# Second sweep of a two-layer graph network: one edge scalar moves from a one-hot matrix to the turned edge features

## The reference, cut to what matters

```python
w = ssp(edge_attr @ W_f1) @ W_f2 * (ssp(s0 @ W_s1) @ W_s2)
w1, w2, w3, w4 = jnp.split(w, 4, axis=-1)          # 128 columns each
x0e, x1e = split_irreps(x[edge_src])               # 128, and 3 x 128
sh0, sh1 = (edge_sh[:, 0], edge_sh[:, 1:4])        # 1 and 3 scalars of the edge
out0 = w1 * x0e * sh0[:, None] + w4 * (jnp.einsum('eum,em->eu', x1e, sh1) / jnp.sqrt(3.0))
out1 = w2[:, :, None] * x0e[:, :, None] * sh1[:, None, :] + w3[:, :, None] * x1e * sh0[:, None, None]
out = jax.ops.segment_sum(merge_irreps(out0, out1), edge_dst, num_segments=N)
```

## Time and profile before

| | |
|---|---|
| time, median of 3 runs | 1228.67 us (1228.24 to 1230.1) |
| profiled execution: its own time, its span | 1229.83 us, 1228.1 us |
| busy share of the span: PE, PEld, DVE, ACT, POOL | 81%, 52%, 70%, 43%, 64% |
| second sweep alone, 700 to 1100 us: PE, DVE, ACT, POOL busy | 396.21, 350.98, 241.75, 278.65 us of 400 |
| granted PE clock there | 1.00 |

### The profile page before, as it was taken

The page is one execution under the profiler, slowest core; times in us unless marked ns, Lnnn a source line. Parts: engine busy times, 40 slices in busy tenths (PEclk is TensorE's granted clock), DMA queues, the critical chain, the costliest instruction groups (busy, mean ns, idle before and its releaser), DMA issues. The chain is left out here.

```text
span 1228.1 us, 23671 instructions
## 1 busy us (share of the span) xinstructions
PE 995.1 (81%) x5530; PEld 642.5 (52%) x5531; DVE 854.4 (70%) x2190; ACT 533.3 (43%) x1559; POOL 780.0 (64%) x809
## 2 busy tenths in 40 slices
PE   2316556199999996756999999999999999999974
PEld 1213232055555554643666666666666666666653
DVE  7351101177778775744888888888888888888857
ACT  2203121023222333543665666656566555666631
POOL 3777777577777760116676776767667676676721
PEclk9757668699999997886999999999999999999987
DMA  9201011277877780125545545455454555545302
GB/s 346 76 15 33 25 32 50 75 238 238 242 240 241 240 218 17 60 94 180 171 156 165 163 153 171 150 167 161 157 170 148 170 159 159 166 150 167 127 1 86
DMA packets 109167, 177.46 MB, mean 145 GB/s; under 512 B 40191, under 2 KB 79343, under 8 KB 109009
## 3 DMA queue, kind: packets, MB, share of 16 engines
q0 software_dynamic: 33184, 130.15, 33.5%
q1 hardware_dynamic: 72752, 45.60, 12.4%
q10 hardware_dynamic: 3200, 1.38, 0.5%
HBM read 157.31 MB, written 19.74 MB: 144 GB/s over the span
## 5 line engine op out<-in xcount | busy, mean ns | idle before, releaser
L1038 POOL TENSOR_TENSOR dot<-ring,ed 128x768 f32<-128x768 f32 x88 | 129.6, 1473 | 134.1 <-issue 109.8
L698 PE MATMUL ps<-ring,aw 128*128 128x512 f32 x352 | 195.6, 643 | 17.7 <-DVE aw L649 16.3
L1028 POOL DMA_INDIRECT ring<-tab_d,ed x176 | 170.4, 968 | 62.2 <-issue 30.5
L618 POOL DMA_INDIRECT ring<-xt_d,ed x176 | 167.5, 952 | 61.4 <-issue 42.0
L375 POOL DMA_INDIRECT slots_d<-stage,stage_pos x157 | 153.5, 978 | 66.3 <-issue 48.7
L1067 PE MATMUL ps<-mm_sb,ohs 128*128 128x512 f32 x352 | 189.1, 619 | 1.4 <-DVE acc L1197 1.4
L1069 PEld LDWEIGHTS ps<-mm_sb,ohs 128*128 128x128 f32 x1056 | 145.6, 191 | 84.2 <-issue 84.2
L1122 ACT ACTIVATE ohs<-oh,ed 128x128 f32<-128x128 f32 x528 | 172.6, 394 | 0.0
L1152 ACT ACTIVATE S_sb<-ps 128x512 f32<-128x512 f32 x176 | 95.5, 595 | 134.6 <-PE ps L1109 134.6
L1069 PE MATMUL ps<-mm_sb,ohs 128*128 128x128 f32 x1056 | 146.2, 275 | 0.0
L1175 DVE TENSOR_TENSOR ps<-S_sb,ps 128x1024 f32<-128x1024 f32 x88 | 108.2, 1229 | 28.0 <-ACT S_sb L1152 26.8
(11 more groups left out here) (194 smaller groups left out, 1859.0 us busy)
## 6 DMA issues: line engine op xcount, KB each, us to landing
ilb<-f_d SPq DMA_DIRECT2D x88, 128.0 KB, 3.8
ed<-slots_d SPq DMA_DIRECT2D x176, 38.0 KB, 3.8
tab_d<-tabrow SPq DMA_DIRECT2D x5, 896.0 KB, 3.7
slots_d<-fill SPq DMA_DIRECT2D x8, 418.0 KB, 4.3
f_d<-ft SPq DMA_DIRECT2D x88, 38.0 KB
ring<-xt_d,ed POOLq DMA_INDIRECT x176, 4.0
hcat<-f_d SPq DMA_DIRECT2D x176, 16.0 KB, 3.8
ring<-tab_d,ed POOLq DMA_INDIRECT x176, 4.4
```

The costliest lines, as they stand in the source:

```text
L618: gp.indirect_dma_start(xg[:, c, k, :], None, xt_d[:, :], bass.IndirectOffsetOnAxis(ap=ed[:, c, k, JD:JD + 1].bitcast(I32), axis=0))\
L698: pe.matmul(ps[:, 2 * u, :], aw[:, r, k, :], xg[:, c, k, 0:D], start=(k == 0), stop=(k == 1))
L1028: gp.indirect_dma_start(xj[:, r, k, :], None, tab_d[:, :], bass.IndirectOffsetOnAxis(ap=ed[:, c, k, JD:JD + 1].bitcast(I32), axis=0))\
L1038: gp.tensor_tensor(dot[:, u, :, :, :], xj[:, r, :, P:D].rearrange("p k (m n) -> p k m n", m=3), ed[:, c, :, IL + 2:IL + 5].unsqueeze(3).to ...
```

## The change

- The scalar `sh0` leaves the one-hot. SP now also loads `s0b`, the turned scalar of each edge spread over 32 rows, and loads `hcat` in one transfer instead of two. A new DVE stage `scaled_features` (lag 2, first in the list) multiplies the turned features by it into `hs0`.
- The columns of `w2` are put in the order w1, w3, w2, w4, in 16 small loads instead of 4 (`NLOADS` 20 to 32). `factors` makes the first 256 columns of F from `hs0` and the last 256 from `hcat`: two matmuls of 512 columns and four of 256.
- `messages` has four steps: the w1 and w2 parts as before, then the inner term (in place in `psF`), then the w3 part, then an addition of the inner term to the first 128 columns.
- `sums` uses the plain one-hot for the 512 columns and drops the separate matmul of 128 columns for the inner term. DVE no longer builds `ohs[..., 0, :]`.

```diff
-        ohs = sb("ohs", [P, 2, 2, SH, P], scope=sweep2)
+        s0b = sb("s0b", [P, U, P], scope=sweep2)
+        hs0 = sb("hs0", [P, 2, P], scope=sweep2)
+        ohs = sb("ohs", [P, 2, 2, SH - 1, P], scope=sweep2)
...
-                        load(w2[HID * q:HID * q + HID, :], W_s2 if q < 2 else W_f2)
+                        w_ = W_s2 if q < 2 else W_f2
+                        for to, fro in ((0, 0), (1, 2), (2, 1), (3, 3)):
+                            load(w2[HID * q:HID * q + HID, P * to:P * to + P], w_[:, P * fro:P * fro + P])
...
-                    for k in range(2):
-                        sp.dma_start(hcat[HID * (k + 2):HID * (k + 3), c, :], turned[k, 0:EA, :]).then_inc(ed2[c], 16)
+                    sp.dma_start(hcat[2 * HID:P, c, :], turned[:, 0:EA, :]).then_inc(ed2[c], 16)
+                    sp.dma_start(s0b[2 * HID:P, c, :], turned[:, IL + 1, :].unsqueeze(1).to_broadcast([2, EA, P])).then_inc(ed2[c], 16)
...
-                        pe.matmul(psA, ohs[:, u, k, 0, :], mm_sb[:, u, k, 0:D], start=(k == 0), stop=False)
+                        pe.matmul(psA, oh[:, u, k, :], mm_sb[:, u, k, 0:D], start=(k == 0), stop=False)
                         for m in range(3):
-                            pe.matmul(psA[:, P * (m + 1):P * (m + 2)], ohs[:, u, k, m + 1, :], mm_sb[:, u, k, D:D + P],
-                                      start=False, stop=False)
-                        mm = pe.matmul(psA[:, 0:P], oh[:, u, k, :], mm_sb[:, u, k, D + P:D + 2 * P], start=False, stop=(k == 1))
+                            mm = pe.matmul(psA[:, P * (m + 1):P * (m + 2)], ohs[:, u, k, m, :], mm_sb[:, u, k, D:D + P],
+                                           start=False, stop=(k == 1 and m == 2))
...
+                    pe.wait_ge(hs_ready, g + 1)
...
-                        mm = pe.matmul((psS if q < 2 else psF)[:, q % 2, :], hcat[rows, c, :], w2[rows, :], start=True, stop=True)
+                        if q < 2:
+                            pe.matmul(psS[:, q, :], hcat[rows, c, :], w2[rows, :], start=True, stop=True)
+                        else:
+                            pe.matmul(psF[:, q - 2, 0:2 * P], hs0[rows, u, :], w2[rows, 0:2 * P], start=True, stop=True)
+                    for q in range(2, 4):
+                        rows = slice(HID * q, HID * q + HID)
+                        mm = pe.matmul(psF[:, q - 2, 2 * P:D], hcat[rows, c, :], w2[rows, 2 * P:D], start=True, stop=True)
...
-                    v.tensor_tensor(mm_sb[:, u, :, 0:D + P].rearrange("p k (s n) -> p k s n", n=P)[:, :, 0:5:4, :],
-                                    psF[:, :, 0:2 * P].rearrange("p k (s n) -> p k s n", n=P),
+                    v.tensor_tensor(mm_sb[:, u, :, :].rearrange("p k (s n) -> p k s n", n=P)[:, :, 0:5:4, :],
+                                    psF.rearrange("p k (s n) -> p k s n", n=P)[:, :, 0:3:2, :],
                                     xj[:, r, :, 0:P].unsqueeze(2).to_broadcast([P, 2, 2, P]), ALU.mult)
+
+                    v.wait_ge(dot_ready, g + 1)
+                    v.tensor_tensor(psF[:, :, 3 * P:D], psF[:, :, 3 * P:D], dot[:, u, :, 0, :], ALU.mult).then_inc(t_done, 1)
                     v.tensor_tensor(mm_sb[:, u, :, P:D].rearrange("p k (m n) -> p k m n", m=3),
-                                    psF[:, :, 2 * P:3 * P].unsqueeze(2).to_broadcast([P, 2, 3, P]),
+                                    psF[:, :, P:2 * P].unsqueeze(2).to_broadcast([P, 2, 3, P]),
                                     xj[:, r, :, P:D].rearrange("p k (m n) -> p k m n", m=3), ALU.mult)
-                    v.wait_ge(dot_ready, g + 1)
-                    v.tensor_tensor(mm_sb[:, u, :, D + P:D + 2 * P], psF[:, :, 3 * P:D], dot[:, u, :, 0, :], ALU.mult).then_inc(msg_ready, 1)
+                    v.wait_ge(t_done, g + 1)
+                    v.tensor_tensor(mm_sb[:, u, :, 0:P], psF[:, :, 3 * P:D], mm_sb[:, u, :, 0:P], ALU.add).then_inc(msg_ready, 1)
...
-                        v.tensor_scalar(oh[:, u, k, :], iota[:, :], ed[:, c, k, IL:IL + 1], None, ALU.is_equal)
-                        ins = v.tensor_scalar(ohs[:, u, k, 0, :], iota[:, :], ed[:, c, k, IL:IL + 1], ed[:, c, k, IL + 1:IL + 2],
-                                              ALU.is_equal, ALU.mult)
+                        ins = v.tensor_scalar(oh[:, u, k, :], iota[:, :], ed[:, c, k, IL:IL + 1], None, ALU.is_equal)
...
+                def scaled_features(g, c, n):
+                    u = c % 2
+                    v.wait_ge(ed2[c], n * 64)
+                    after(v, f_ready, g - 1)
+                    v.tensor_tensor(hs0[2 * HID:P, u, :], hcat[2 * HID:P, c, :], s0b[2 * HID:P, c, :], ALU.mult).then_inc(hs_ready, 1)
...
-                pipelined(v, (3, one_hot), (3, weights), (3, messages), (2, softplus), (0, turned_one_hot), (4, accumulate),
+                pipelined(v, (2, scaled_features), (3, one_hot), (3, weights), (3, messages), (2, softplus), (0, turned_one_hot), (4, accumulate),
```

More of the change, by code:

```diff
@@ L230, in batches @@
                 embed(q)
-        NLOADS = 20
+        NLOADS = 32
         loads = [0]
@@ L968, in build @@
         dot = sb("dot", [P, 2, 2, 3, P], scope=sweep2)
-        mm_sb = sb("mm_sb", [P, 2, 2, D + 2 * P], scope=sweep2)
+        mm_sb = sb("mm_sb", [P, 2, 2, D + P], scope=sweep2)
         ed2 = [sem(f"ed2_{c}") for c in range(U)]
@@ L991, in build @@
         w_done = sem("w_done")
+        hs_ready = sem("hs_ready")
+        t_done = sem("t_done")
         dot_ready = sem("dot_ready")
@@ L1121, in step @@
                         for k, m in which:
-                            ins = act.activation(ohs[:, u, k, m, :], oh[:, u, k, :], ACT.Copy, scale=ed[:, c, k, IL + 1 + m:IL + 2 + m])
+                            ins = act.activation(ohs[:, u, k, m - 1, :], oh[:, u, k, :], ACT.Copy, scale=ed[:, c, k, IL + 1 + m:IL + 2 + m])
                         if which[-1] == (1, 3):
```

## The result

The changed kernel takes 1213.61 us (median of 4 runs, 1212.89 to 1215.25) against 1228.7 us before (4 runs): 0.9877 of the time, interval 0.9862 to 0.9893, or 15.1 us less. The forecast was 1203.5 us, with a range of 1192 to 1218: the direction and the range held, the gain is 0.6 of the one predicted. The profiled execution took 1213.61 us, with a span of 1211.9 us (1228.1 before).

A forecast was written before the change was run, and what follows sets the result against it. Tied paths through PE's sums were taken to set 6.92 us an iteration; then a two-iteration path over DVE, 6.62: 0.30 x 87 = 26 us less, 1202.6, put at 1203.5 for mutual delays; range 1192 to 1218.

The forecast's parts named there:

- path A: One-iteration path inner, sums, accumulate, products, next inner: 6.93 us, called the pace before; 6.49 after the change.
- Path C: Two-iteration path: factors, ACT's copy of S, DVE's list, PE to the next-but-one factors: 13.24 us before, 13.23 after.
- Path E: Not predicted, drawn up later: inner, half 0 of sums, ACT's log steps, register read, accumulate, products: 6.92 before, 6.70 after.
- rival 2: The six matmuls of factors hand over badly, some 0.3 to 0.44 us: about 1213 to 1224 us; chance 0.12.
- rival 3: The row strips in factors no longer run side by side, adding 0.88 us: 1268 us; chance 0.06.
- D: Path of DVE's list of steps alone, one iteration: 5.91 us before, 5.92 after, no bound.
- rival 4: DVE and POOL block each other at scaled_features: 6.95 us an iteration, about 1231 us, no gain; chance 0.05.
- Rival 1: Only PE counts; the pace falls with sums alone by 0.44 to 0.55 us: 1181 to 1191 us; chance 0.07.

The follow-up runs named there:

- e5: The kernel before with the register read for accumulate moved ahead of weights: 1226.32 us, 0.9963 of the kernel before.
- e1: The changed kernel with the register read for accumulate moved ahead of weights: 1204.77 us, 0.979 of the kernel before.
- e3: The changed kernel with the register read moved ahead of weights and turned_one_hot moved behind products: 1193.49 us, 0.970 of the kernel before.
- e6: The kernel before with the 16 small loads of w2 in the old column order: 1230.51 us, 0.9998 of the kernel before.
- e8: The changed kernel with one more matmul of 128 columns in half 1 of sums: 1217.14 us, 0.9902 of the kernel before.
- e11: The kernel before with ACT's first log step (Abs) done twice: 1243.67 us, 1.0101 of the kernel before.
- e12: The changed kernel with early register read, turned_one_hot behind products and an own semaphore for the edge rows: 1191.09 us, 0.9674 of the kernel before.
- e9: The changed kernel with ACT's first log step (Abs) done twice: 1226.87 us, 0.9976 of the kernel before.
- e2: The changed kernel with turned_one_hot moved from ahead of accumulate to behind products: 1206.42 us, 0.9804 of the kernel before.
- e4: The changed kernel without the DVE addition of the inner term: 1211.7 us, 0.9846 of the kernel before.
- e7: The changed kernel with one more matmul of 128 columns in half 0 of sums: 1232.48 us, 1.0017 of the kernel before.
- e10: The changed kernel with the register read ahead of weights and ACT's first log step (Abs) done twice: 1200.29 us, 0.9754 of the kernel before.

## Why the prediction was right in sign and range, and wrong in size

*The step that failed* is the list of paths. "This path is the pace", said of path A, and "C takes over", said of the changed kernel, held only among the four paths listed, and none of them goes through ACT's log steps and the register read: what the read costs ahead of `accumulate` stood at nothing. The choice of A rested on the releaser printed beside `accumulate`, [0.46 <-PE ps L1071] in the earlier trace rows. That row names the wait of the instruction that came last by its semaphore, and the register read ahead of it, in the sequencer's rows, wasn't looked at. In the kernel before the two ended close together: the last L1071 ends by the model at 902.62, 0.17 before `accumulate`; the read's last row (SEQ_ASSERT) starts at 902.5, and one more register operation follows, as after the change. e5 says how close: without the read the pace falls by 0.05 us. After the change, counted from the end of the log, half 1 of `sums` ends 0.23 earlier (903.08 - 902.45 = 0.63 for 902.62 - 901.76 = 0.86), and `accumulate` still starts at 1.04 for 1.03, since the read takes as long as before. Path E, 6.70, stays above C, and the 0.22 of half 1 becomes idle time. 0.22 x 87 = 19 us is the gain inside the sweep (19.3 measured), where 0.30 x 87 = 26 stood in the sum. The start of the sweep, below, takes back another 4.2.

*That the range held is luck.* The forecast's own stretch was 1194 to 1211, and 1213.61 lies above it. The range reached up to 1218 only to take in a part of rival 2, and the bad hand-over of that rival did not happen.

*Path C* held as a sum. From the rows of the changed kernel it is 2.36 from `factors` (903.71) to `weights` (906.07), 4.13 to `accumulate` (910.20), 0.60, 1.01 and 5.31 (905.10 to 910.41): together 13.41, but for rounding the 13.40 of two iterations, with a gap of 0.21 ahead of `accumulate` in it (0.52 against 0.31 in e1). Without the gap, 13.19 / 2 = 6.60; e1 measured 6.594 and 1204.77 us, what had been forecast (6.62 and 1203.5) for the change itself. e3, which takes 0.31 more off C, gains 0.115 of the 0.155 that C gives. That C sets the pace in e1 rests on these two sums; no run adds a step to it there. Of the signs forecast for C, e1 shows that DVE no longer waits there and that PE waits for `products`. That `weights` waits longer than 0.32 for ACT's copy did not come: 0.19 on average in the changed kernel, 0.29 in e1.

*The terms.* Two matmuls, 0.22 each: right for half 0 (1.84 to 1.62), and for PE's stretch from `inner` to the next `factors` (5.77 to 5.31). `factors` with six matmuls: taken as 0.1, it measured 0.04 (1.21 to 1.25), so rivals 2 and 3 fell. PE's rows show why: L1122 starts at 904.26, 0.53 after L1119, as before the second four followed the first at 0.51. The Trainium skill, "TensorE: Matmul & The Clock Gate", Part 3 ("What overlaps and what doesn't"), says that a weight load overlaps a running matmul only on another row strip; by the prediction's estimate that would have made it 0.3 to 0.4. The trace does not agree, with 0.04. The addition and the inner term in place: 0.33 each, right. `scaled_features` takes 0.29 us (median of 88 is 290 ns) and 0.32 from its start to the next step's, for 0.20 in the sum of D, which set nothing. In the timeline POOL is at rest beside it, so rival 4 fell; the first of the 88, at 565.5 beside a POOL step of 1.47, took 0.69. The loads: 0, right (e6).

*Rival 1*, only PE counts, fell to e8: there PE does one matmul more in each iteration for 0.02 us.

*What the sum did not have* is the start of the sweep. The first `accumulate` comes 4.2 us later. SP's first load of the sweep and the first gather on POOL, after, then before:

```profile
550.66 0.37 SPq L1016 DMA_DIRECT2D ed<-slots_d  x1
556.54 0.98 POOL L1034 DMA_INDIRECT ring<-tab_d,ed  x1 [21.49 <-DMA s0b<-f_d]
```

```profile
550.51 0.37 SPq L1010 DMA_DIRECT2D ed<-slots_d  x1
555.21 0.98 POOL L1028 DMA_INDIRECT ring<-tab_d,ed  x1 [20.32 <-DMA hcat<-f_d]
```

The load is issued 0.15 later, and from it to the gather are 5.88 us for 4.70, 1.2 more: the first gathers wait for `s0b`, which shares a semaphore with `ed`. In the four kernels with the edge loads of before (before, e5, e6, e11) these are 4.6 to 4.7 us, in the nine with the shared wait 5.7 to 5.9, and in e12, where the gathers wait for `ed` alone, 2.69. So this part is the wait's. The larger part, 3.0 us, lies between the first `products` and the first `accumulate` (21.75 us for 18.72), where the granted clock differs. Windows of 8 us (length, busy us of PE, PEld, DVE, ACT, POOL, clock, DMA share, GB/s), after and before:

```profile
576.00:584.00 8.00, 6.76 (x32) 4.75 (x34) 6.47 (x13) 3.13 (x10) 5.60 (x7) 0.57 0.50 158
```

```profile
576.00:584.00 8.00, 7.96 (x56) 4.84 (x53) 7.15 (x15) 4.41 (x14) 5.61 (x6) 1.00 0.62 193
```

After the change PE ran most of these 8 us at 1.2 GHz and not at 2.4, with gaps ahead of it: it had waited 1.32 us for `softplus` at 577.24, where it waited 0.83 at 575.75 before. All 14 kernels fall into three groups by the clock granted in the 8 us from 12 us behind the first `products`: where it is 1.00 (before, e3, e5, e6, e9, e11, e12), the first `accumulate` follows the first `products` by 18.3 to 19.1 us; where it is 0.79 (e1, e2, e4, e7, e8), by 20.0 to 20.4; where it is 0.57 (the changed kernel, e10), by 21.75. e3 and e9 have the shared wait and the full clock, so the wait alone does not bring the clock down; what does so was not tried.

## What to carry to other kernels

A closed path must be followed through the sequencers too: ahead of an instruction that waits, look for register reads on its engine, and for the wait behind which they stand. Where a stall ends with a releaser, compare that releaser's end with the start: the gap left tells whether something else ended at nearly the same time, and a gain is then worth only the distance to it. To learn which path is the pace, add a known small step to one place at a time; e7 and e8 told in two runs what no view of the profile did. A step that costs nothing shows that its place is off the path only as far as the next path's slack: in e8 C had caught up.

## What the runs showed of the hardware that was not expected

- Reading a number from SBUF into a register of DVE's sequencer: the load takes 0.30 us, but from its first operation to the start of the instruction that uses it are 0.9 us (902.6 to 903.49, with two other steps of DVE under way in them), and it began only when the wait of `softplus` ahead of it was over (901.9 behind a log that ended at 901.76 before, 902.6 behind 902.45 after). Moved to where the sequencer had time, it was worth 0.10 us an iteration (e1 against the changed kernel: 6.698 to 6.594).
- Two stationary operands one after the other on a row strip cost 0.04 us more than one (`factors` to ACT's copy, 1.21 to 1.25 us), where each passes over 256 columns in place of one over 512.
- While the sweep's pipeline filled, PE ran most of 8 us at 1.2 GHz in the changed kernel (0.57 granted), in a stretch where the kernel before had 1.00. In the two kernels with 0.57 the first `accumulate` came 2.7 to 3.5 us later behind the first `products` than in the seven with 1.00.
